# A scan kernel's row plan: the shared stages at other steps, stores by block, and small projections in halves

## The reference

```python
u = layernorm(x)                                  # over channels
xh, z = split(u @ W_in)                           # 512 and 512 channels
xc = depthwise_conv3x3(xh, conv_k)
xp = xc @ W_xproj                                 # dt_r (8), B (16), C (16)
dt = softplus(xp[:8] @ W_dt + b_dt)
dtN = dt @ W_dtN + b_dtN                          # 16
for t in range(48 * 48):                          # the scan, over the tokens of an image
    h = exp(dt_t * A) * h + (dtN_t * B_t) * x_t   # h: 512 channels x 16 states
    y_t = sum_n(h * C_t) + Dskip * x_t
x = x + (layernorm(y) * ln_g + ln_b) * silu(z) @ W_out + b_out
t = layernorm(x)                                  # the "ffn": a byte shift decoded from channels
x = x + t + 2 * one_hot(low nibble) at 64..79 + 2 * one_hot(high nibble) at 72..87
```

## Time and profile before

| | us |
|---|---|
| median of 3 runs | 4036.85 |
| lowest and highest | 4023.55, 4038.51 |
| the profiled execution | 4022.24 |
| its span, first to last instruction | 4020.4 |
| first step's L869 begins at | 116.3 |
| last step's L869 begins at | 3981.4 |

### The profile page before, as it was taken

How to read it: one execution, slowest core, us unless ns; L and a number is a source line. 1 busy time by engine, 2 the same in 40 slices (tenths; PEclk the granted TensorE clock), 3 DMA queues, 4 the chain that set the end, 5 groups by cost and what they waited for, 6 DMA issues and landing times.

```text
span 4020.4 us, 103342 instructions
## 1 busy us (share of the span) xinstructions
PE 3251.8 (81%) x33792; PEld 1589.3 (40%) x33792; DVE 3622.2 (90%) x12317; ACT 2944.1 (73%) x6050; POOL 3133.2 (78%) x5771
## 2 busy tenths in 40 slices
PE   5788888888888888888888888888888888888665
PEld 2334433443344334433443344344433343444333
DVE  2799999999999999999999999999999999999996
ACT  3677777777777787777777777777777777787663
POOL 0788877888888788877888788778877888788874
PEclk7889887889889988988898889888888798889776
DMA  3877878788878787878787878787877888788773
GB/s 67 219 202 203 213 191 206 190 208 205 208 196 214 199 211 196 215 194 205 197 216 199 207 196 213 199 205 193 206 201 199 201 203 209 202 206 205 192 192 80
DMA packets 383392, 790.26 MB, mean 197 GB/s; under 512 B 80517, under 2 KB 235142, under 8 KB 382854
## 3 DMA queue, kind: packets, MB, share of 16 engines
q1 hardware_dynamic: 382854, 783.66, 77.1%
HBM read 648.18 MB, written 96.73 MB: 185 GB/s over the span
## 4 chain that ended last, share of the span: by engine, by line
DVE 31%; PE 31%; ACT 26%; issue 7%; SPq 3%; POOL 2%; DMA 1%; ACTq 0%; POOLq 0%; DVEq 0%
ACT ps_a L638 8%; PE ps_s L583 6%; DVE h L885 6%; PE ps_y L492 6%; PE ps_s L528 4%; DVE ps_a L869 4%; DVE ps_a L872 4%; DVE h L888 4%; PE ps_s L537 3%; ACT ap L648 3%; PE ps_s L566 3%; PE ps_y L476 2%; ACT y L721 2%; DVE sz L941 2%; PE ps_s L584 2%
## 5 line engine op out<-in xcount | busy, mean ns | idle before, releaser
L638 ACT ACTIVATE ps_a<-dtb,a_n 128x384 f32<-128x384 f32 x2304 | 1253.6, 583 | 488.1 <-DVE h L888 472.3
L1169 POOL TENSOR_TENSOR h<-mp,up 128x128 f32<-128x128 f32 x2304 | 1052.5, 457 | 357.6 <-PE ps_y L492 147.4
L1159 POOL TENSOR_TENSOR mp<-ap,h 128x128 f32<-128x128 f32 x2304 | 1051.9, 457 | 358.1 <-ACT ap L648 242.7
L869 DVE TENSOR_TENSOR ps_a<-ps_a,h 128x192 f32<-128x192 f32 x2304 | 813.6, 353 | 239.6 <-ACT ps_a L638 236.7
L885 DVE SCALAR_TENSOR_TENSOR h<-xb,db,ps_a 128x192 f32<-128x192 f32 x2304 | 921.9, 400 | 24.0 <-PE ps_y L492 16.0
L888 DVE SCALAR_TENSOR_TENSOR h<-xb,db,ps_a 128x192 f32<-128x192 f32 x2304 | 927.2, 402 | 0.0
L492 PE MATMUL ps_y<-h,cw 64*32 64x256 f32 x18432 | 787.9, 461 | 71.9 <-DVE h L888 58.0
L872 DVE TENSOR_TENSOR ps_a<-ps_a,h 128x192 f32<-128x192 f32 x2304 | 807.7, 351 | 0.0
L648 ACT ACTIVATE ap<-dtb,a_n 128x256 f32<-128x256 f32 x1152 | 524.2, 509 | 251.1 <-DMA dtb<-xd 233.9
L1149 POOL TENSOR_TENSOR up<-xb,db 128x512 f32<-128x512 f32 x576 | 610.8, 1060 | 3.0 <-DMA xb<-xd 3.0
L492 PEld LDWEIGHTS ps_y<-h,cw 64*32 64x32 f32 x18432 | 315.7, 122 | 488.2 <-DVE h L888 244.6
(11 more groups left out here) (111 smaller groups left out, 4286.5 us busy)
## 6 DMA issues: line engine op xcount, KB each, us to landing
xb<-xd SPq DMA_DIRECT2D x576, 512.0 KB, 7.2
dtb<-xd SPq DMA_DIRECT2D x576, 512.0 KB, 6.3
xs<-xh SPq DMA_DIRECT2D x196, 192.0 KB, 6.2
xd<-dttok SPq DMA_DIRECT2D x288, 128.0 KB, 5.4
xin<-in_x_dram SPq DMA_DIRECT2D x144, 128.0 KB, 6.2
xd<-xtok SPq DMA_DIRECT2D x192, 96.0 KB
res<-in_x_dram SPq DMA_DIRECT2D x144, 128.0 KB, 5.4
out_dram<-res SPq DMA_DIRECT2D x144, 128.0 KB, 3.9
```

The costliest lines, as they stand in the source:

```text
L638: ins = act.activation(ps_a[buf][:, n, 0:2 * VD].rearrange("p (t d) -> p t d", t=2), dtb[:, u % DUNITS, 2 * buf:2 * buf + 2, 0:VD], ACT.Ex ...
L869: dve.tensor_tensor(a[:, 0], a[:, 0], last[:, 0], ALU.mult).then_inc(m0_done, 1)
L1159: pool.tensor_tensor(mp[:, G % 2], ap[:, Q % 2, G % 4], h[:, (G - 1) % HRING, :, VD:HALF], ALU.mult) \
L1169: pool.tensor_tensor(h[:, G % HRING, :, VD:HALF], mp[:, G % 2], up[:, Q % 2, G % 4], ALU.add) \
```

## The change

It moves stages to other steps and changes the form of some. On the plan: conv of row i+2, not i+1, is done in steps 40 to 43 of row i, xproj in step 1; proj moves from the row's end into the next row's steps 0, 2, 10 and 11; dtp is done in two pairs, in steps 3 and 21; xtok in 6, 7 and 9; the transposes of y in 16 to 19, the gates in 18 to 21 (before 21 to 24), out in 23 to 25 (before 29 to 31), z in 27 to 30, dtn in 31, dttok in 32, 33 and 35. finish_dt stands in steps 13 and 26 on GpSimd (before 16 and 17). The ffn of row i-2 is done in steps 0 to 13 of row i, one stage to a step, in 12 stages.

On the form: xp and dbt are kept as two halves of the row's tokens, on partitions 0 to 63 and 64 to 127. xproj, dtp and dtn become pairs of matmuls over 192 columns, xproj and dtn in two column halves of PE, dtp in two row halves. bounce_states issues four transfers, not two. store_x and store_dt are issued by block. The ffn drops the comparison of hot with 0.5 and two small operations, and marks and weighs both nibbles in one instruction each.

```diff
 SLOT = {
-    "conv": (0, 1, 3, 4), "xproj": (6,), "dtp": (8, 9, 11, 12), "xtok": (14, 15, 16), "yt": (18, 19, 20, 21),
-    "dttok": (23, 24, 26), "dtn": (27,), "out": (29, 30, 31), "z": (33, 34, 36, 37), "xlnT": (39, 40),
-    "proj": (42, 43, 45, 46),
+    "proj": (0, 2, 10, 11), "xproj": (1,), "dtp": (3, 3, 21, 21), "xtok": (6, 7, 9), "yt": (16, 17, 18, 19),
+    "out": (23, 24, 25), "z": (27, 28, 29, 30), "dtn": (31,), "dttok": (32, 33, 35), "conv": (40, 41, 42, 43),
+    "xlnT": (45, 46),
...
-                    if s == 6 and exists(i - 2):
+                    if s in (8, 10, 12) and exists(i + 1):
+                        store_x(i + 1, (8, 10, 12).index(s))
+                    if s == 13 and 0 <= i + 3 <= SIDE:
+                        load_stack(i + 3)
+                    if s == 14 and exists(i - 2):
                         store(i - 2)
-                    if s == 8 and 0 <= i + 3 <= SIDE:
-                        load_stack(i + 3)
-                    if s == 18 and exists(i - 1):
+                    if s == 19 and exists(i - 1):
                         load_residual(i - 1)
-                    if s == 21 and exists(i + 1):
-                        store_x(i + 1)
-                    if s == 26 and exists(i + 1):
-                        store_dt(i + 1)
-                    if s == 30 and exists(i + 1):
+                    if s == 34 and exists(i + 1):
                         bounce_states(i + 1)
-                    if s == 34 and exists(i + 1):
+                    if s in (35, 36, 38) and exists(i + 1):
+                        store_dt(i + 1, (35, 36, 38).index(s))
+                    if s == 37 and exists(i + 1):
                         load_states(i + 1)
-                    if s == 42 and exists(i + 5):
+                    if s == 47 and exists(i + 5):
                         load_xin(i + 5)
...
-                    mm = pe.matmul(bank[0:XP_ROWS, 0:TOK], wxp[:, g, :], by_step(xc[:, r % 2, g, :]),
-                                   start=g == 0, stop=g == NG - 1)
+                    for half in range(2):
+                        lo = half * XP_ROWS
+                        mm = pe.matmul(bank[lo:lo + XP_ROWS, 0:HTOK], wxp[:, g, :],
+                                       by_step(xc[:, r % 2, g, :])[:, half * QUADS // 2:(half + 1) * QUADS // 2],
+                                       start=g == 0, stop=g == NG - 1, skip_group_check=True)
...
+                banks = [take_bank("dtp", r, 2 * pair + half) for half in range(2)]
+                for n in range(2):
+                    g = 2 * pair + n
+                    for half in range(2):
+                        rows = slice(half * XP_ROWS, half * XP_ROWS + DTR + 1)
+                        mm = pe.matmul(banks[half][:, n * HTOK:(n + 1) * HTOK], wdt[rows, g * P:(g + 1) * P],
+                                       xp[rows].rearrange("p b w -> p w b"), start=n == 0, stop=n == 1,
+                                       skip_group_check=True)
...
-                    if s in (30, 31, 32):
-                        add_residual(i - 1, s - 30)
+                    if s in (24, 25, 26):
+                        add_residual(i - 1, s - 24)
...
-                    if s == 28:
+                    if s == 33:
                         make_db(i + 1)
...
-                    ins = dve.tensor_scalar(hot[:], hot[:], 0.5, None, ALU.is_gt)
+                    for w in range(3):
+                        ins = dve.scalar_tensor_tensor(score[:, :, w, :], hot[:, :, 32 + 8 * w:48 + 8 * w], 0.5,
+                                                       score16[:].unsqueeze(1).broadcast_to([P, KT, 16]),
+                                                       ALU.is_gt, ALU.mult)
```

274 lines of the change are left out of this document (139 added, 135 removed).

## The result

The changed kernel takes 4393.93 us (median of 4 runs, 4391.91 to 4396.07), the kernel before 4030.20 beside it on the same chip: 1.090 times as long, 95% interval 1.0873 to 1.0931. The sign was as forecast, the size was not: 4106 was given, with a range up to 4220. The profiled execution has a span of 4392.7 us; before it was 4020.4.

What follows compares the result with a forecast made beforehand. It took DVE, with its waits, to bound the kernel: 73.2 work + 4.4 + 0.9 + 2.1 + 1.6 = 82.2 us a row against 80.76, +69 us over 48 rows, giving 4106 us; range 3940 to 4220.

Steps and rivals of the forecast that it cites:

- The old waits go: DVE's 5.6 us a row of waits in the kernel before, mostly for ACT's decay, were counted as removed.
- A: Steps 24 to 26: add_residual moves earlier and waits for the residual (SP) and out (PE); costs 4.4 us a row.
- R3: Rival: PE at half clock from the fourth gate on slows out, skip, sum and conv; 4250 us; chance 0.15.
- C: Step 44: four convs stand between the sums of steps 40 and 44, so DVE waits 2.1 us a row.
- SP's half of step A: SP's queue: residual loaded only after out's stores land, arriving about 42.3 us into the row, 3.6 us late.
- B: Step 32: z's four parts stand between out and dtn, so the next sum ends 0.9 us late.
- D: Row's end: later dt stores delay the next row's first dtb load and its decays; adds 1.6 us a row.
- DVE's work: Falls from 75.2 to 73.2 us a row: 1.7 us from the ffn, 0.3 from make_db.
- R4: Rival: a halved matmul doesn't run beside its other half, out begins 1 us later; 4154 us; with forecast 0.42.
- R1: Rival: waits are planned away, the added terms shrink to some 2 to 5 us together; 3856 to 3940 us; chance 0.29.
- R2: Rival: new waits just eat what was won, no change; 4000 to 4055 us; chance 0.14.
- The start and the end: First row's conv and last ffn, outside the steady rows: taken as 0, with 15 us either way.

Runs made afterwards that it cites:

- e5: Changed kernel with extra PE matmuls to unread columns in steps 13, 16, 18 and 19, five more behind step 19's transposes: 4339.82 us.
- e10: Changed kernel with extra PE matmuls in steps 16, 18, 19 and 20, second dtp pair moved from step 21 to 13: 4225.66 us.
- e6: Changed kernel with out in steps 24 to 26, behind the skip and sum of step 24, its adding in 25 to 27: 4208.58 us.
- e8: Changed kernel with another plan from step 23 on: out in 25, 26, 28, dtn 29, z 33 to 39, conv 41, 42, 44, 45: 3942.55 us.
- e2: Changed kernel with conv's four parts in steps 40, 41, 44 and 45 instead of 40 to 43: 4260.08 us.
- e13: e2 with ACT's copies of conv's parts two steps behind the part, not one: 4329.67 us.
- e11: Kernel before with only the new form of the ffn, in its old place, two stages to a step in steps 40 to 45: 4044.97 us.
- e15: Changed kernel with every stage of the ffn one step later, form unchanged: 4270.14 us.
- e12: e8 with two buffers for res and the residual loaded in step 5: 3921.23 us.
- e9: e5 with dtp reading 64 rows instead of 9, the added rows of wdt zero: 4292.34 us.

## Why the prediction was wrong, step by step

**The old waits go: right for their places, wrong as a term.** The waits for the decay at steps 10, 16 and 18 are gone, 3.4 us a row. But the prediction put DVE's waits from ACT's own work at nothing, and its sign, waits for the decay nearly gone, failed: they are 4.6 us a row, as before. It had counted ACT's work between two decays, and not that this work (copies of z and conv) waits for PE or DVE with the decay behind it in the list.

**A, steps 24 to 26, 4.4 us forecast, 7.85 measured.** This is the main step that failed. The order of events was right: gates, out's first part, skip, sum, third part. The sum took out's part at 2.55 us and the rest at full clock. The fourth gate ended at 2275.93 - 2237.26 = 38.7 us into the row (forecast 36.0 to 37.6), the sum at 47.4 (forecast 41 to 42.4), because what lay between took 8.7 us and not 4.8. So the term was mis-sized by 3.45 us: it priced the skip, the sum and out at full clock. Rival R3 had the mechanism, its place and its price (2.2 to 5 us; e5's rows measure 3.8, e10 3.5), and its condition, half clock for over 3 us from the fourth gate on, held in nearly every row. It was given 0.15 on the ground that transposes and two sums precede and had brought the clock back in the kernel before; here the dtp pair and a pause of 1.6 us (3 in eleven rows) stood between them and out. R3's own time was too low by its own prices: 82.2 + 2.2 to 5 in A + 1.8 in C are 86.2 to 89.0 us a row, 4298 to 4432 us, which holds the 4394; it wrote 84.5 to 86 and 4250, and the range was cut off at 4220 by that. But e6 shows that the clock alone is not the cause: with the sum ahead of out, at half clock until then, steps 24 to 28 wait 4.0 us instead of 7.85. Order and clock share one loss; e6 wins 3.9 us a row and e10 3.5, and they can't be added. Another 0.8 us of the 7.85 is the wait for the decay at step 24, which the prediction had not counted.
SP's half of step A gave the residual's landing as 42.3 us into the row, and 42.3 it was on the average, but partly by luck: the terms as written add up to 41.7, its issue ended at 38.2 and not at 36.3, and it landed 4.1 us later and not 5.4. For DVE it was wrong: D24 came at 41.1 us in this row (41.7 on the average), not at 38.1, 1.2 of it by the wait for the decay and the rest by the ffn and the statistics ahead of it, which put D8 at 16.4 and not 15.1. The residual was late by about 1 us, and out was later still; DVE waits for it once PE is out of the way, 0.9 us a row in e10 and 0.4 in e8.

**B, step 32: the right number, 1.1 us against 0.9, by luck.** The sum, which the term was made of, cost 0.3; the other 0.9 is the decay behind ACT's reads of z, which the prediction had at nothing.

**C, steps 40 to 44, 2.1 us forecast, 4.25 measured.** Four convs took 7.95 us, as forecast. Two things were left out. ACT's list: the decays of steps 42 and 44 stand behind copies that wait for conv, 3.0 us a row. e2, where the sum's wait goes and the decay's stays, and e13, where a later copy takes the decay's wait from step 42, show it. And the half clock again: skip and sum took 3.6 us at step 40 where 2.1 were counted. The start of the skip was put at D36 + 1.6; it was at D36 + 2.5.

**D, the row's end: nothing, 1.6 forecast.** The last dt store left at D36 + 7.2 (forecast 6.5, though its terms, -3.0 + 10.1, make 7.1) and was there at D36 + 10.3 on the average, 3.1 us later and not 5.4; and the next row began only at D36 + 19.4, since it was already longer by C. No wait for dtb stands at the row's start.

**DVE's work, 73.2 us forecast, 75.4 measured.** make_db gave 0.2 us (610 to 406 ns), near the 0.3 forecast. The ffn's 1.7 did not: the lower bound was 0.8 for the case that the scores wait for GpSimd, and e11 has 0.3. The step that failed here is that bound: it let two passes of each pair vanish at their mean, whereas the time of a pass that meets GpSimd's product is mostly that of the product, and when one pass is taken away or shifted another meets the product (e15's lines show it). In the plans where GpSimd stands at the scores the work is 73.9 (e2) and 73.5 (e8), near the forecast.

**R4 did not hold**, the halves run side by side. xproj and dtn took 1.52 us each where whole ones took 2.81 and 2.78; dtp took 2.10 + 2.20 against 5.76, a gain of 1.5 and not 2.7. No drain at either end can be seen. None of it moved the time, as the sum said.

**R1 and R2** held the opposite error, waits smaller than forecast. Other plans bring them only to about the 5.6 us of before, 5.5 in e8 and 5.1 in e12; that they can be planned away as far as R1 had it, no run shows.

The sum with what was measured: 75.4 + 7.85 + 1.1 + 4.25 + 0 = 88.6 us a row (88.75 by the window). Against the forecast's 82.2 that is 3.45 more from A, 2.15 from C, 0.2 from B and 2.2 from DVE's work, and 1.6 less from D. The start and the end gave 11 us, inside the 15.

## What to carry to other kernels

When a stage that waits for a slow producer is moved in an in-order list, look first at what stands behind it and is awaited by the engine that bounds the kernel: the same stage one step later, behind the sum, cost 3.9 us a row less. Price every move of PE's work at either level of its clock, and where one rival multiplies several terms of the sum at once (skip, sum, out and conv alike), don't leave it at the chance of a single mishap. A transfer or an early load is worth nothing while something else is later, and its worth appears when that is gone.

## What the runs showed of the hardware

- PE's clock fell to half 0 to 1.5 us after eight matmul pieces of nine rows, although PE had been busy and at full clock until they ended (e5, in 27 of forty rows, for 10.2 us). In twelve rows of the same run, with the same pieces and the same pause behind them, it did not fall. With 64 rows instead, equally long, it fell in 12 rows for that long and in 8 for less (e9). So the rows of the pieces are part of it, and the rest is open.
- The half clock ahead of an awaited stage cost 3.8 us of a row by e5's own rows, 88.9 against 85.0 us. In e8 PE was at half clock for 17.1 us a row and out was waited for no more than 0.4 us.
- dtp's pieces took 2.10 us at full clock and 2.20 at half, so they are not bound by that clock; out's took 1.99 and 3.78.
- A DVE instruction on few columns with two inputs took from 199 ns (e2) to 558 ns (the kernel after) and 591 ns (e11) on the average, form unchanged, by what GpSimd did beside it. Moving the ffn by one step took it from one line and gave it to another (e15).
- A shift of one step in DVE's list went with a halved stretch of PE's clock of 17.1 us instead of 23.9, in 39 of forty rows (e15); the way from the one to the other is not shown.
